# A two-layer routed FFN with a gated mixer between: twelve code bodies for the expert products, from 144 columns, in place of six from 240

## What is computed

```python
x = x + 0.5 * ffn(layernorm(x), gate_weight, wi, wo)
x = x + mixer(layernorm(x), ...)
x = x + 0.5 * ffn(layernorm(x), gate_weight, wi, wo)

def ffn(tokens, gate_weight, wi, wo):        # 8 experts, hidden 512, inner 2048
    logits = tokens @ gate_weight.T
    top1 = argmax(logits)                    # one expert per token
    # an expert takes its first 320 tokens, the rest are dropped
    hmid = gelu(dispatch @ wi[e])            # (tokens of e) x 512 @ 512 x 2048
    eout = hmid @ wo[e]                      # (tokens of e) x 2048 @ 2048 x 512
    out  = prob * eout, back in the tokens' order
```

## Time and profile before

| | before |
|---|---|
| median of 3 runs | 1204.99 us (1200.31 to 1214.65) |
| the profiled execution | 1213.92 us |
| its span, first to last instruction | 1212.2 us |
| TensorE busy | 1065.3 us, 88% of the span |
| VectorE / ScalarE busy | 736.6 / 566.4 us, 61% / 47% |
| mean granted TensorE clock | 0.945 |

### The profile page before, as it was taken

The page is one execution under the profiler, slowest core; times in us unless marked ns, Lnnn a source line. Parts: engine busy times, 40 slices in busy tenths (PEclk is TensorE's granted clock), DMA queues, the critical chain, the costliest instruction groups (busy, mean ns, idle before and its releaser), DMA issues.

```text
span 1212.2 us, 20879 instructions
## 1 busy us (share of the span) xinstructions
PE 1065.3 (88%) x7658; PEld 988.6 (82%) x7658; DVE 736.6 (61%) x1199; ACT 566.4 (47%) x871; POOL 127.6 (11%) x140
## 2 busy tenths in 40 slices
PE   5479796999999999579999993999999999789895
PEld 2169796999999999557778751999999999789895
DVE  6536454676667768458776854557767767545451
ACT  4335343555455656245343242445656556434341
POOL 3500101010100101100000014001101101010100
PEclk9779898999999999889999996899999999989898
DMA  9775833475454753230000035554755647524410
GB/s 272 241 244 212 292 117 137 140 263 206 142 195 160 282 198 126 69 92 1 1 35 35 1 113 200 196 183 138 251 181 208 208 172 261 195 94 136 149 69 22
DMA packets 90330, 189.05 MB, mean 156 GB/s; under 512 B 4592, under 2 KB 5104, under 8 KB 90224
## 3 DMA queue, kind: packets, MB, share of 16 engines
q1 hardware_dynamic: 84272, 169.50, 41.2%
q0 software_dynamic: 6016, 18.97, 4.1%
HBM read 160.02 MB, written 32.62 MB: 159 GB/s over the span
## 4 chain that ended last, share of the span: by engine, by line
PE 74%; DMA 8%; issue 6%; ACT 3%; POOL 3%; DVE 2%; SPq 2%; DVEq 0%; ACTq 0%; POOLq 0%
PE psH L1062 11%; PE psH L1063 11%; PE psH L1064 11%; PE acc L1069 9%; PE acc L1071 9%; PE acc L1070 9%; DMA raw_wi<-in_wi 5%; PE acc L1062 3%; PE acc L1063 3%; PE acc L1064 3%; POOL disp L456 2%; DMA disp<-zeros 2%; PE psT L1205 1%; PE acc L1161 1%; PE psH L1161 1%
## 5 line engine op out<-in xcount | busy, mean ns | idle before, releaser
L1062 PE MATMUL psH<-dth,wih 128*128 128x240 f32 (+5 forms) x1024 | 298.3, 291 | 8.8 <-issue 7.0
L1069 PE MATMUL acc<-hth,woh 128*128 128x240 f32 (+5 forms) x1024 | 294.2, 287 | 6.4 <-DVE htl L734 6.4
L1063 PE MATMUL psH<-dtl,wih 128*128 128x240 f32 (+5 forms) x1024 | 296.1, 289 | 0.0
L1064 PE MATMUL psH<-dth,wil 128*128 128x240 f32 (+5 forms) x1024 | 295.8, 289 | 0.0
L1070 PE MATMUL acc<-htl,woh 128*128 128x240 f32 (+5 forms) x1024 | 293.2, 286 | 0.0
L1071 PE MATMUL acc<-hth,wol 128*128 128x240 f32 (+5 forms) x1024 | 293.1, 286 | 0.0
L734 DVE TENSOR_TENSOR wol<-raw_wo,woh 128x1024 fp32r<-128x1024 f32 x128 | 156.3, 1222 | 133.8 <-ACT woh L576 133.8
L1062 PEld LDWEIGHTS psH<-dth,wih 128*128 128x128 f32 x1024 | 195.9, 191 | 11.9 <-issue 10.5
L576 ACT ACTIVATE woh<-raw_wo 128x1024 fp32r<-128x1024 f32 x128 | 135.4, 1059 | 146.0 <-PE acc L1071 144.0
L596 ACT ACTIVATE gel<-psH 128x320 f32<-128x320 f32 x256 | 111.0, 437 | 196.4 <-PE psH L1064 193.5
L1069 PEld LDWEIGHTS acc<-hth,woh 128*128 128x128 f32 x1024 | 192.8, 188 | 8.0 <-DVE htl L734 8.0
(11 more groups left out here) (160 smaller groups left out, 1181.8 us busy)
## 6 DMA issues: line engine op xcount, KB each, us to landing
raw_wi<-in_wi SPq DMA_DIRECT2D x64, 1024.0 KB, 6.5
raw_wo<-in_wo SPq DMA_DIRECT2D x64, 1024.0 KB, 6.9
dtok<-disp SPq DMA_DIRECT2D x16, 516.0 KB, 3.9
disp<-zeros SPq DMA_DIRECT2D x4, 1287.5 KB, 21.1
out_x<-xt SPq DMA_DIRECT2D x4, 1024.0 KB, 4.8
xt<-in_x SPq DMA_DIRECT2D x3, 1024.0 KB, 13.0
xt<-x SPq DMA_DIRECT2D x3, 1024.0 KB, 12.0
dtok<-disp SPq DMA_DIRECT2D x16, 129.0 KB, 4.3
```

The source lines that it names most:

```text
L1062: pe.matmul(out, lh, rh, start=first, stop=False)
L1063: pe.matmul(out, lh, rl, start=False, stop=False)
L1064: return pe.matmul(out, ll, rh, start=False, stop=last)
L1069: pe.matmul(out, lh, rh, start=False, stop=False, skip_group_check=True)
```

## The change

One line. The list of widths begins at 144 in place of 240, still in steps of 16:

```diff
-WIDTHS = range(240, CAP + 1, 16)
+WIDTHS = range(144, CAP + 1, 16)
```

## The result

| | before | after |
|---|---|---|
| median | 1208.50 us (1200.31 to 1214.65, 4 runs) | 1358.51 us (1351.67 to 1365.65, 4 runs) |
| the profiled execution | 1213.92 us | 1351.67 us |
| its span | 1212.2 us | 1350.0 us |
| mean granted TensorE clock | 0.945 | 0.87 |

A forecast was written before the change was run, and what follows sets the result against it. TensorE, busy 88% of the span, mostly with the six product lines, was taken to bound the kernel. From a median of 1205.0 us, -4.6 (narrower matmuls) + 34.6 (stalls) + 12.3 (tests) gave 1247 us, range 1222 to 1282.

The forecast's parts named there:

- The failed step: Clock staying low through the narrow experts: named only as what would make the forecast wrong, without size or chance.
- Narrower matmuls: In seven experts' products, columns below 240 buy next to nothing: 4.6 us saved, bounds nothing and 47 us.
- Five new stalls: Between experts, first use of each narrower width per layer must fetch its code: 34.6 us added, bounds 19 and 48.
- More tests: Longer row of compare-and-branches in visit and run between experts: 82 exposed tests at 0.15 us, 12.3 us added.
- Rival 1: Between experts, blocks beyond the five are lost (288, 224, 192 coming back): three more at 7.2 us, 1269 us, 25%.
- Rivals 3 to 5: 3: fetches hidden, 1215 us, 4%; 4: also columns counting below 240, 1173, 2%; 5: no body below 240 taken, 1217, 1%.

The follow-up runs named there:

- experiment 1: Changed kernel with twelve bodies and tests, but no body working on fewer than 240 columns: 1294.78 us, ratio 1.0748 to the kernel before.
- experiment 2: Changed kernel with bodies of 144, 160 and 176 working on 192 columns: 1295.59 us, ratio 1.0725 to the kernel before.
- experiment 3: Kernel before, its 240-column body working on 176 columns, slots beyond left out, no added pause: 1211.08 us, ratio 1.0001.
- experiment 5: Kernel before, smallest body at 176 columns, plus 24 never-true tests ahead of each run dispatch as a pause: 1561.22 us, one execution.
- experiment 6: Kernel before, smallest body at 192 columns, plus 24 never-true tests ahead of each run dispatch as a pause: 1282.38 us, one execution.
- experiment 8: Kernel before with six never-true tests added ahead of both dispatches of each expert: 1225.53 us, ratio 1.0147.
- experiment 10: Kernel before with three widths (240, 288, 320) in both layers: 1202.2 us, ratio 0.9975.
- experiment 11: Kernel before with two widths (240, 320) in both layers: 1204.74 us, ratio 0.999.
- experiment 12: Kernel before with widths 240, 288, 320 in the first layer and 240, 320 in the second: 1190.59 us, ratio 0.9863.
- experiment 4: Changed kernel with every body below 240 working on 176 columns, slots beyond left out: 1391.81 us, one execution.
- experiment 7: Kernel before, its 240-column body working on 144 columns, slots beyond left out, no added pause: 1219.41 us, one execution.
- experiment 9: Kernel before with six never-true tests ahead of both dispatches, plus never-entered bodies of 144 to 224 columns in the code: 1261.58 us, ratio 1.045.

## Why the prediction was right in sign and wrong in size

**The failed step: the clock inside the narrow experts, put at nothing.** The sum of the forecast had a term for the low clock in the stretches between experts, and none for the clock in the products behind them. The last sentence of the prediction names that case and gives it neither a price nor a chance, "no row of before shows that case". It held more than the whole forecast of 42 us: 73.4 us in experts 12 and 13, 63 us by experiments 1 and 2. The price could have been estimated: the earlier trace rows shows the stream at 240 columns bound by its weight loads, and if a weight load at half the clock takes twice as long (0.21 us it was), one expert costs some 40 us more when the clock stays low. With seven such experts that would have been a bound of 280 us. The rival was in sight, and it was left out because the trace had no row for it, which is a reason for a wide range and not for a chance of nothing. Which condition brings it about is shown by one change in each direction: 176 columns without a pause (experiment 3), 176 with one (experiment 5), 192 with one (experiment 6).

**Narrower matmuls: right.** Forecast 4.6 us saved, bounds 0 and 47. Experiments 1 and 2 differ by 0.8 us, far inside their intervals, where seven experts have 16 to 48 columns less; experiment 3 has 64 less in eight experts and a ratio of 1.0001. The saving is nothing that can be measured. The 0.0017 us taken off the distance was the difference between a count in a window (20/179) and the starts of two loads as printed (0.11), and not a gain: the same count gives 180 loads in 20 us at 240 columns and at 192. The reading of the earlier trace rows, that a load behind idle time takes 0.11 us whatever follows, was the one that carried.

The Trainium skill states the floor in other terms: "TensorE: Matmul & The Clock Gate", section "LDWEIGHTS (loading the stationary operand)", puts a weight load at its columns over 1.2, which is 107 ns for 128 columns. The 0.110 to 0.112 us of all widths from 144 to 240 agree with it at a granted clock of 1.00; at 0.50 the distance was 0.21 us. The 81 ns for a pair, from the section that the prediction weighed, was not reached in these products at any width.

**Five new stalls: right in place, too small in price.** All five long branches came where they were forecast, at 260.8, 854.9, 914.9, 1016.1 and 1109.7 us, on line 1229. The five stretches grew from 16.7 us together to 57.5, 40.8 us, against 34.6. The stretches ahead of experts 10 and 12 stand out, with 9.9 and 10.6 us more. Ahead of 10 the join stalled as well (909.5 us), ahead of 12 the run behind its visit did (3.29 us at 1026.7), and ahead of 13 too (3.76 us at 1117.6). The step took for granted that one missed branch for each new width is all, and that what a visit has fetched is there for the run. Why it wasn't, no run tests on its own. These run branches matter beyond their own time: they are what put the pause directly ahead of the narrow products.

**More tests: the right size.** Forecast 0.15 us each, 12.3 in all; measured 0.125 by experiment 8, whose 17 to 18 us are for six tests in all sixteen experts, where no stretch was left out. In the changed kernel the stretches ahead of experts 6, 7 and 11, which have no stall, grew by 1.8, 1.5 and 0.8 us for 12, 12 and 6 tests: 0.12 to 0.15 us.

**Rival 1, more blocks lost: it came as well.** 288 (315.5 us) and the second 224 (377.2) stalled as it said, with 7.3 and 7.2 us more in their stretches, just the 7.2 of a stall. 192 did not stall a second time. Ahead of the first two stretches 1.3 and 4.0 us came on top, and the leaving of the first layer stalled for the first time, 5.3 us. Against that the two stretches at the end got shorter, by 3.0 and 4.9 us: of the 320s the second now found its code there. So stalls and tests came to 56.8 + 5.3 = 62 us against 46.9. The same sum from the profiled executions of experiments 1 and 2, which have the same branches in the same layout, is 70 and 72 us, and lies partly elsewhere. A stall forecast for one place is therefore good to some 7 us and the sum to some 10; which blocks are lost is not settled by the order of branches alone. (The layout is `join` thirteen blocks behind the head's block, seven before; fourteen and eight count the head's block in, as the prediction does.)

On how much stays the Trainium skill ("Runtime: NRT & Kernel Launch", section "Instruction fetch mechanics") gives 2048 instructions, eight blocks, for TensorE. No run bears out eight: with head, three bodies and join, five blocks (of which it uses four, 288 being taken by none of its experts), the second layer of experiment 10 still stalls at the second 320, and only with two bodies (experiments 11 and 12) is it free of stalls between experts. The same section's rule that a taken branch to a block outside the current two waits for its fetch agrees with the 3.2 to 7.7 us of each missed branch here, but two can't be all that stays either: experiment 11 loops over head, two bodies and join without a stall between experts.

**Rivals 3 to 5** did not come: the first visit of each new width stalled itself, for 3.5 to 6.1 us, and the narrow bodies were taken.

## What to carry to other kernels

Before narrowing a moving operand, count weight loads in a window: if the distance is the load's own, here 0.11 us at every width from 144 to 240, fewer columns buy nothing. Price what happens if the clock falls as a narrow stream begins: at 176 and 160 columns it stayed at half speed for the whole stream, so a pause directly ahead of one cost not its own 3 us but 37 more. And each variant of a body picked at run time costs tests, blocks and fetches for all the others; let each loop have the few variants that its data use, which is what made the fastest kernel here.

## What the runs showed of the hardware

- Behind 2.6 to 3.5 us without a weight load directly ahead of 384 matmuls, each with a weight load of 128 columns, the granted clock fell to 0.5 around the first matmuls and did not come back before the last, in all thirteen such experts of 176 or 160 columns (80.3 to 81.8 us for what takes 44 at 1.0: the changed kernel, experiments 4 and 5). At 192 columns behind such pauses it was back after 3.4 to 6.8 us (experiments 2 and 6). The same 176 columns without the pause keep 1.0 (experiment 3); behind a longer pause (9.4 us) that had the turning of tokens after it, in which the clock came back, they do too (experiment 4). Where between 176 and 192 columns the line lies is open.
- Such a pause does not always bring a fall: behind 2.8 us ahead of expert 3 in experiment 1, at 240 columns, the clock stayed at 1.0. Within products of 144 and 176 columns 1.3 to 1.9 us were enough four times (experiments 3 and 7), each time less than 5 us before their end, and the clock was back only after it; other waits of 1.0 to 1.5 us there brought none.
- A missed taken branch on TensorE lasted 3.2 to 7.7 us, and an expert boundary with one took some 7 us more than one without; a test that falls through costs 0.125 us.
- Code that is never entered cost 36 us (experiment 9 against 8), through where it puts the code around it.
